# Four places for the row numbers of results, and the wait for the preceding scatter moved from the sum to the scatter

## The reference

```python
logits = 30 * tanh((x @ w_gate) / 30)          # 1024 rows, 8 experts
probs = softmax(logits)
weights = probs * mask_of_the_two_largest
for e in range(8):
    h = silu(x @ w1[e]) * (x @ w3[e])          # 256 -> 512
    out = out + h @ w2[e] * weights[:, e:e+1]  # 512 -> 256
x = layernorm(x + out)
```

## Time and profile before

| what | value |
|---|---|
| three runs | 772.64, 773.75, 778.9 us (median 773.75) |
| profiled execution, span from first to last instruction | 771.2 us |
| time of the profiled execution around its span | not listed for itself; the median of the runs is 2.55 us above the span |
| busy: PE, PEld, DVE, ACT, POOL | 651.9, 530.4, 484.2, 436.5, 209.7 us |
| mean granted TensorE clock | 0.949 |
| first load of expert rows issued | 608.40 us |
| last scatter landed | 749.6 us |

### The profile page before, as it was taken

How to read it: one execution, slowest core, us unless ns; L and a number is a source line. 1 busy time by engine, 2 the same in 40 slices (tenths; PEclk the granted TensorE clock), 3 DMA queues, 4 the chain that set the end, 5 groups by cost and what they waited for, 6 DMA issues and landing times.

```text
span 771.2 us, 13774 instructions
## 1 busy us (share of the span) xinstructions
PE 651.9 (85%) x4748; PEld 530.4 (69%) x4749; DVE 484.2 (63%) x1091; ACT 436.5 (57%) x1123; POOL 209.7 (27%) x364
## 2 busy tenths in 40 slices
PE   6788788998999999868878999999986299999960
PEld 4566577998988989834556676868875277777740
DVE  1577766577586576477836756565555576776735
ACT  3988846457556556457767646465442256556522
POOL 2454510040010010011213334344237223332324
PEclk9999999999999999999999999999998599999985
DMA  8995000220220220061020000000095111111114
GB/s 302 377 325 157 1 1 1 86 86 1 87 86 1 86 86 1 1 240 33 1 83 1 1 2 2 1 2 1 5 416 225 59 29 54 41 48 48 46 47 145
DMA packets 31921, 62.02 MB, mean 80 GB/s; under 512 B 2452, under 2 KB 26776, under 8 KB 29624
## 3 DMA queue, kind: packets, MB, share of 16 engines
q1 hardware_dynamic: 29848, 56.04, 21.4%
q0 software_dynamic: 2016, 5.22, 1.9%
HBM read 45.80 MB, written 15.55 MB: 80 GB/s over the span
## 4 chain that ended last, share of the span: by engine, by line
PE 46%; ACT 20%; DVE 15%; DMA 8%; issue 5%; POOL 4%; SPq 1%; POOLq 0%; ACTq 0%; DVEq 0%
PE banks L1725 25%; PE bank L1725 21%; ACT arena L741 5%; DVE U_split L1204 4%; ACT arena L1009 4%; DMA ys<-arena 4%; DMA arena<-xs 3%; ACT U_split L760 2%; DVE mx L1158 1%; DVE dmx L1486 1%; POOL arena L665 1%; ACT arena L1016 1%; POOL rstd L549 1%; POOL xs L645 1%; ACT arena L779 1%
## 5 line engine op out<-in xcount | busy, mean ns | idle before, releaser
L1725 PE MATMUL banks<-U_split 128*128 128x512 f32 (+1 forms) x616 | 148.9, 354 | 4.8 <-DVE U_split L1204 1.9
L1725 PE MATMUL bank<-U_split 128*128 128x256 f32 (+1 forms) x864 | 113.6, 287 | 15.3 <-DVE U_split L1204 15.2
L1725 PEld LDWEIGHTS bank<-U_split 128*128 128x128 f32 x864 | 106.7, 191 | 19.6 <-issue 15.0
L1725 PEld LDWEIGHTS banks<-U_split 128*128 128x128 f32 x616 | 97.1, 190 | 22.5 <-issue 7.5
L760 ACT ACTIVATE U_split<-arena 128x1024 fp32r (+6 forms) x122 | 97.1, 821 | 22.7 <-PE banks L1725 10.9
L1725 PE MATMUL banks<-cst,arena 128*128 128x128 f32 (+1 forms) x594 | 87.3, 278 | 19.2 <-DMA arena<-xs 16.0
L546 POOL TENSOR_SCALAR rstd<-mv 128x1 f32<-128x1 f32 x48 | 11.8, 247 | 298.1 <-DVE mv L1136 266.3
L1725 PE MATMUL banks<-arena 128*128 (+4 forms) x632 | 84.8, 382 | 8.3 <-ACT arena L1009 5.0
L1725 PEld LDWEIGHTS banks<-cst,arena 128*128 128x128 f32 (+1 forms) x594 | 68.4, 141 | 33.2 <-issue 13.6
L1009 ACT ACTIVATE arena<-banks,dmx 128x128 f32<-128x128 f32 (+1 forms) x128 | 52.2, 420 | 53.8 <-DVE dmx L1486 53.8
L622 POOL TENSOR_SCALAR arena<-arena,dri 128x128 f32<-128x128 f32 (+1 forms) x128 | 52.9, 434 | 91.7 <-DVE dri L1454 91.7
(11 more groups left out here) (225 smaller groups left out, 1162.7 us busy)
## 6 DMA issues: line engine op xcount, KB each, us to landing
arena<-in_w_exp SPq DMA_DIRECT2D x8, 1536.0 KB, 14.2
xs<-arena SPq DMA_DIRECT2D x8, 1032.0 KB, 14.2
arena<-in_ctxT SPq DMA_DIRECT2D x4, 1601.0 KB, 6.8
arena<-in_ctx SPq DMA_DIRECT2D x4, 1536.0 KB
arena<-in_w_f SPq DMA_DIRECT2D x3, 1024.0 KB, 11.8
arena<-xs SPq DMA_DIRECT2D x23, 129.0 KB, 2.0
w_x<-in_w_x SPq DMA_DIRECT2D x9, 256.0 KB, 7.7
arena<-in_w_oh SPq DMA_DIRECT2D x1, 2048.0 KB, 8.0
```

What stands on the lines that cost most here:

```text
L1725: return nc.tensor.matmul(o, w, x, start=start, stop=stop, **k)
```

## The change

`y_ids` has four places in place of two, and tile i uses place i mod 4. The sum of tile i waits no longer for the scatter of tile i-2 but for that of tile i-4, the last reader of its place. The wait for the preceding scatter, which only the last scatter had of its own, now stands in front of every scatter but the first. All else, the load of rows with its own two waits included, is as it was.

```diff
+Y_IDS = 4
...
-        y_ids = late.cut(2, dt=U32)
+        y_ids = late.cut(Y_IDS, dt=U32)
...
             def m_ids(i):
 
-                slot = i % 2
+                slot, place = i % 2, i % Y_IDS
                 pool.wait_ge(G[f"m_x{slot}"], 16 * (i // 2 + 1))
-                if i >= 2:
-                    pool.wait_ge(G[f"m_st{slot}"], 16 * (i // 2))
-                g.tensor_scalar(y_ids[:, slot:slot + 1], xg[:, slot, E:E + 1], xg[:, slot, E + 1:E + 2], None, ALU.add).then_inc(G["m_ids"], 1)
+                if i >= Y_IDS:
+                    pool.wait_ge(G[f"m_st{slot}"], 16 * ((i - Y_IDS) // 2 + 1))
+                g.tensor_scalar(y_ids[:, place:place + 1], xg[:, slot, E:E + 1], xg[:, slot, E + 1:E + 2], None, ALU.add).then_inc(G["m_ids"], 1)
 
 
             m_ids(0)
             for i in range(TILES):
-                slot = i % 2
+                slot, place = i % 2, i % Y_IDS
                 if i + 1 < TILES:
                     m_ids(i + 1)
-                else:
+                if i > 0:
                     pool.wait_ge(G[f"m_st{1 - slot}"], 16 * ((i + 1) // 2))
                 pool.wait_ge(G["m_ids"], i + 1)
                 pool.wait_ge(G["m_y_sb"], i + 1)
-                g.indirect_dma_start(ys, bass.IndirectOffsetOnAxis(ap=y_ids[:, slot:slot + 1], axis=0),
+                g.indirect_dma_start(ys, bass.IndirectOffsetOnAxis(ap=y_ids[:, place:place + 1], axis=0),
                                      yt[:, slot, :], None).then_inc(G[f"m_st{slot}"], 16)
```

## The result

The changed kernel took 769.83 us in the median of its runs, the kernel before 775.65 in the same series; the ratio is 0.9922, with a 95% interval of 0.9896 to 0.9949. Timed a second time beside some of the experiments it was 0.9882 (0.9847 to 0.9918). At 775.65 us the first ratio is 6.1 us less (4.0 to 8.1); predicted were 4.9, and 768.9 us. In the second series the medians lie further apart, 774.75 and 766.58, which is 8.2 us, though the steps of the stage are the same to 0.01 us; the steps account for 6.1, and where the rest comes from no run here tells.

A forecast was written before the change was run, and what follows sets the result against it. The expert stage was taken as bound by scatter, sum and row load at 5.67 us per step; 18 steps at 5.40 make 97.2 in place of 102.06, so 773.75 - 4.9 = 768.9 us, range 764.5 to 772.0.

The forecast's parts named there:

- the ring through scatter, sum and load: Expert stage: result, scatter, sum, row load and transposes bound the kernel before, 11.36 us per two tiles, 5.67 per step.
- the second ring: Expert stage: gate, silu, high part, low part, low part of the rows, next gate; 5.40 us, seen bare at 5.30.
- the ring through ACT and DVE: The same as the second ring; sets the step after the change at 5.40 us, not PE's 5.14.
- PE's rival: Expert stage: PE's own 5.14 to 5.16 us per step becomes the bound, 9.2 us less, 764.5 us; chance 9%.
- gate to silu: Link from a tile's gate on PE to silu on ACT, taken as 1.79 us of the 5.40.
- The sum behind the scatter: POOL's sum of row numbers starts 1.36 us behind the scatter's start and takes 0.29, or 0.95 beside DVE.
- Cover of the rows: Rows loaded for a tile are there 0.5 to 1.2 us before PE asks for them.
- Wait at the scatter at nothing: 21 more scatters wait for the preceding one on POOL; cost zero, covered by 2 us and more.
- The slower rivals: Load and scatter hold each other up: 1 to 7 us slower, 777.6, 7%; sum holds up DVE: 774.1 us, 5%.

The follow-up runs named there:

- the number read first: Changed kernel, with ACT reading the next tile's expert number ahead of its wait for the gate: 5.16 us per step, ratio 0.9875; second time 5.17, 0.9850.
- A delay of 0.7: Changed kernel with 24 small fills of an unused tile on POOL in front of each sum: 5.33 us per step, no wait of PE for rows.
- one of 1.1: Changed kernel with 44 small fills on POOL in front of each sum: 5.66 us per step without one of 7.45, ratio 0.9983.
- the two kernels with the late ring back: Changed kernel with the waits of before (5.68 us per step without one of 9.39, ratio 1.0001), and with 44 fills before each sum (5.66, ratio 0.9983).

## Why the prediction was right

- *The stage was bound by the ring through scatter, sum and load*: shown. Only the waits were changed back in one kernel, and 5.68 came back; the load was made late in another, and 5.66 came back. The prediction had the second ring bare in tile 2's step alone; in fact six of the 18 gates before already followed DVE's low part, at no cost that the trace shows, since PE waited for rows behind them.
- *Next is the ring through ACT and DVE, not PE*: shown, by its links in the trace, and by the number read first, which shortened a link of that ring alone, and the step with it. PE's rival at 764.5 us was 0.2 us per step away.
- *Size of that ring*: 5.40 predicted, 5.34 measured. The term off is gate to silu: I took 1.79 for all steps; it is 1.78 in every other one (653.02 to 654.80) and 1.70 in those between. What makes the two differ isn't settled. It is most of the 97.2 - 96.17 = 1.0 us by which the 18 steps came out shorter. From tile 3's gate to tile 22's the gain is 6.1, and 4.9 were predicted; the 0.2 beyond that 1.0 are tile 21's step, which I left at 5.34. Behind it the stage's end is as before.
- *The sum behind the scatter*: predicted start 1.36, measured 1.23, by two errors that partly cancel: the gap is 0.05 and not the 0.31 between two indirect transfers, and the scatter's own 1.18 is longer than the 1.05 taken. Duration 0.29, as taken.
- *Cover of the rows*, predicted 0.5 to 1.2 us: 5.83 - 4.47 = 1.4 by the rows' lengths, but in truth less. A delay of 0.7 is free, one of 1.1 is not, since the sum then meets DVE's low part, which starts 2.3 to 2.4 behind the scatter in the changed kernel. I had weighed the collision for the place of the sum, and not as what ends the cover.
- *Wait at the scatter at nothing*: each of the 18 scatters was released by ACT's result, none by a scatter.
- *The slower rivals*: loads beside a scatter's end took 1.9 to 2.1 us, as before, and DVE's low part of the first matrix started 1.20 to 1.21 behind ACT's high part in every step, so nothing held it up.

## What to carry to other kernels

When a wait leaves a ring, the gain is set by the next longest ring, and a step in which the old wait happened to be absent (here tile 2's) shows it bare. A small instruction on POOL can be three times as long beside a DVE instruction with two inputs in SBUF; count it at its long duration while it stands there, and ask where it will stand after the change. A register read between two instructions of ACT put their starts 0.21 us further apart here, twice the gap of 0.11 that the trace shows between them, since it also took away their overlap; the step got 0.18 from it.

## What was not expected of the hardware

POOL's indirect transfer lasted 1.16 to 1.20 us in the steps of tiles 4 to 20 of the changed kernel, where its first 0.24 to 0.28 ran beside DVE's low part of the second matrix (653.40 to 654.62), and 1.04 with the number first, where only 0.03 did (680.81 against an end at 680.84). The kernel before has both kinds, from 1.04 to 1.19. In these two, every transfer of the steps of tiles 2 to 20 that began 0.15 or more ahead of the end of that low part ended 0.91 to 0.93 behind it, however early it had begun. So DVE's end, and not the transfer's own start, sets when such a one is over; the mechanism is not shown.

In the two kernels with the late ring back, one load of rows, that of tile 4, took about twice the usual 2.05: 4.03 and 3.74 us. The chain of waits in the first of them, the load with its issue:

```profile
628.60 0.03 issue
628.63 4.03 DMA arena<-xs
632.65 0.04 issue
632.70 1.50 PE banks L1726 x6
```

PE waited 2.69 us for it, and behind that the granted clock fell. Windows of that kernel (busy of PE, PEld, DVE, ACT, POOL, then the clock, DMA share, GB/s):

```profile
630.00:633.00 3.00, 0.54 (x6) 0.30 (x5) 1.84 (x2) 1.58 (x2) 0.65 (x1) 1.00 0.24 77
633.00:638.00 5.00, 5.00 (x18) 4.01 (x17) 2.41 (x4) 1.44 (x2) 0.29 (x1) 0.66 0.10 26
638.00:640.00 2.00, 2.00 (x13) 1.72 (x12) 0.22 (x1) 0.98 (x2) 0.83 (x1) 1.00 0.01 4
```

0.66 over 5 us is a mixture of the two levels, 2.4 and 1.2 GHz; the eight weight loads of `m_down` took 3.08 in it, and 1.71 elsewhere. One late load cost that step 9.39 - 5.67 = 3.7 us. In the other kernel PE waited 2.41 for its rows, the clock stayed at 1.00, and the step was 7.45. Why these loads were slow no run here tells.
